# Second attention's scores in two row halves, the down product in two column halves, the second attention's keys and values in four column strips

## The reference

```python
x = x + L0_xattn(layernorm(x), ctx, ...)        # 16 heads of 16, q and k normalised per head, softmax over 1601 keys
x = x + L0_ffn(layernorm(x), U1, V1, b1, U2, V2, b2)   # 256 -> 64 -> 1024, gelu, -> 64 -> 256
x = x + L1_xattn(layernorm(x), ctx, ctx, mask, ...)    # one head of 16
x = x + L1_ffn(layernorm(x), phi, W, b)         # soft mixture over 64 experts with 32 slots each
```

```python
q = query @ Wq + bq;  k = key @ Wk + bk;  v = value @ Wv + bv
scores = einsum('bqd,bkd->bqk', q, k) / sqrt(256)
scores = (scores - mean(scores)) / (std(scores, ddof=1) + 1e-8)
attn = softmax(scores + where(mask, -1e-32, 0))
head = einsum('bqk,bkd->bqd', attn, v);  out = tile(head, 16) @ Wout + bout
```

## Time and profile before

| | us |
|---|---|
| median of three runs | 6866.95 |
| the profiled execution | 6864.03 |
| its span | 6862.2 |
| TensorE busy | 6307.0 (92%) |
| VectorE busy | 3514.3 (51%) |
| ScalarE busy | 3263.7 (48%) |
| GpSimd busy | 2408.1 (35%) |

### The profile page before, as it was taken

How to read it: one execution, slowest core, us unless ns; L and a number is a source line. 1 busy time by engine, 2 the same in 40 slices (tenths; PEclk the granted TensorE clock), 3 DMA queues, 4 the chain that set the end, 5 groups by cost and what they waited for, 6 DMA issues and landing times. The chain is left out here.

```text
span 6862.2 us, 93027 instructions
## 1 busy us (share of the span) xinstructions
PE 6307.0 (92%) x35933; PEld 3091.1 (45%) x35933; DVE 3514.3 (51%) x6804; ACT 3263.7 (48%) x6001; POOL 2408.1 (35%) x2689
## 2 busy tenths in 40 slices
PE   3799999999999999999999999966999999999999
PEld 1223333333333333333333333226888888666666
DVE  3565665665656656656656566516666666000000
ACT  1366666666666666666666666522222222111111
POOL 4226436346355264363463552342222222000000
PEclk9799999999999999999999999968999999999999
DMA  2442332432432423314324324003444444311110
GB/s 64 77 76 57 67 76 56 73 69 63 76 71 55 84 57 66 78 55 73 69 63 76 70 53 75 6 16 135 157 167 154 158 162 163 121 56 56 49 56 31
DMA packets 364938, 546.09 MB, mean 80 GB/s; under 512 B 59824, under 2 KB 281984, under 8 KB 364240
## 3 DMA queue, kind: packets, MB, share of 16 engines
q1 hardware_dynamic: 321232, 498.18, 30.0%
q10 hardware_dynamic: 43264, 41.95, 1.8%
...
## 5 line engine op out<-in xcount | busy, mean ns | idle before, releaser
L1193 DVE TENSOR_REDUCE mx<-psum 128x1 f32<-128x401 f32 x4096 | 2212.9, 570 | 1615.7 <-PE psum L767 1606.6
L1038 ACT ACTIVATE probs<-psum 128x512 f32<-128x512 f32 (+1 forms) x3328 | 1910.6, 599 | 910.4 <-PE psum L789 907.3
L767 PE MATMUL psum<-kst,qst 96*128 96x401 bf16 x4096 | 1356.6, 343 | 192.5 <-DVE mx L1193 149.6
L789 PE MATMUL psum<-qst,kst 99*128 99x512 bf16 (+1 forms) x3328 | 1286.0, 387 | 49.9 <-ACT probs L1038 44.8
L800 PE MATMUL psum<-probs,vaug 128*17 128x512 f32 x6656 | 886.8, 605 | 0.0
L789 PEld LDWEIGHTS psum<-qst,kst 99*128 99x128 bf16 (+1 forms) x3328 | 328.8, 99 | 1178.5 <-ACT probs L1038 748.9
L767 PEld LDWEIGHTS psum<-kst,qst 96*128 96x128 bf16 x4096 | 402.7, 98 | 962.8 <-DVE mx L1193 756.3
L1460 POOL TENSOR_TENSOR disp<-disp,rz 128x2048 f32<-128x2048 f32 x64 | 294.7, 4605 | 905.5 <-DVE rz L1679 905.5
L1479 PE MATMUL psum<-phi,xT 128*128 128x128 f32 x4096 | 511.0, 279 | 39.1 <-DMA xT<-xnT_scratch 31.8
L1630 ACT ACTIVATE disp<-psum 128x512 f32<-128x512 f32 x256 | 152.8, 597 | 807.6 <-PE psum L1547 807.6
L1479 PEld LDWEIGHTS psum<-phi,xT 128*128 128x128 f32 x4096 | 479.0, 193 | 86.8 <-issue 79.1
...
## 6 DMA issues: line engine op xcount, KB each, us to landing
xnb<-xn_scratch SPq DMA_DIRECT2D x256, 512.0 KB, 3.6
...
y_scratch<-ysb ACTq DMA_DIRECT2D x128, 256.0 KB, 3.3
...
```

Source lines behind the costliest of these rows:

```text
L767: mm(to[:, 0:PW], qst[g][0:NP, j, t * P:(t + 1) * P], kst[g][0:NP, j, k0:k0 + PW], start=True, stop=True).then_inc(m_full, 1)
L789: mm(bank[S_BANK[n % 2]][0:m, :], kst[g][0:NR, j, c * P:c * P + m], qst[g][0:NR, j, :], start=True, stop=True).then_inc(s_full, 1)
L1038: fn(probs[0:m, 4 * (k % 2) + j, :], bank[S_BANK[j % 2]][0:m, :], ACT.Exp, scale=float(HD) ** 0.5).then_inc(s_exp, 1)
L1193: v.tensor_reduce(mx[:, n % 2, u // 4, u % 4:u % 4 + 1], bank[M_BANK[r % 2]][:, 0:PW], AX.X, ALU.max).then_inc(m_free, 1)
```

## The change

Three products of stage one use the array in parts, and the table of `woven` is written anew from step 15 on, with smaller moves in steps 0 to 3.

1. Scores (`s1`): `kv1T` holds the keys twice, in rows 0 to 31 and 64 to 95, and `q1a` the queries twice, in rows 0 to 15 and 64 to 79. One call does two chunks: the even one with rows 0 to 63 into `hb`, the odd one with rows 64 to 127 into `b6`. A call waits for the exponentials of both chunks of the call before. Seven calls take the place of thirteen, the last with one chunk.
2. Down product (`U2`): two hidden chunks in one call, into partitions 0 to 63 and 64 to 127 of `b7`. The two halves are added by the V2 product, which has 128 rows, with V2 loaded twice.
3. Keys and values (`kv1`): four matmuls of 128 tokens for each half of the channels, in four strips of 32 partitions. ScalarE copies 128 x 128 in place of 32 x 512. The sum of the keys lies in four strips, and a new matmul with a selecting matrix `sel` (`km`) adds them up before VectorE's mean (`kmr`). The way back from DRAM is four DMAs in place of one, and GpSimd subtracts the mean from 128 partitions.

```diff
-        put((15.67, 16.34, 17.34, 18.34, 20.0, 21.0, 22.0, 23.0)[f], -1, "U2", f)
...
+    for p in range(FC // 2):
+        put((16.34, 18.34, 21.67, 23.67)[p], -1, "U2", p)
...
-    for c in range(KC):
-        put(35.0 + 0.5 * c, -1, "s1", c)
...
+    for p in range((KC + 1) // 2):
+        put((35.67, 36.67, 38.0, 39.0, 40.34, 41.34, 42.67)[p], -1, "s1", p)
     for k in range(4):
-        put((36.95, 38.95, 40.95, 41.95)[k], -1, "pv1", k)
...
-                (v2[:, :], w["L0_ffn_V2"]),
+                (v2[0:RANK, :], w["L0_ffn_V2"]),
+                (v2[RANK:P, :], w["L0_ffn_V2"]),
...
-                (bkv[0:A1, :], w["L1_xattn_bk"].rearrange("(p a) -> p a", a=1)),
-                (bkv[A1:2 * A1, :], w["L1_xattn_bv"].rearrange("(p a) -> p a", a=1)),
...
+            for j in range(4):
+                loads.append((bkv[32 * j:32 * j + A1, :], w["L1_xattn_bk"].rearrange("(p a) -> p a", a=1)))
+                loads.append((bkv[32 * j + A1:32 * j + 32, :], w["L1_xattn_bv"].rearrange("(p a) -> p a", a=1)))
...
-                    sp.wait_ge(h_full, at("h_full", b - 1, "s1", KC - 1))
+                    sp.wait_ge(h_full, at("h_full", b - 1, "s1", KC // 2))
...
-                sp.dma_start(kv1T[0:2 * A1, :], kv1_d[b]).then_inc(kv1_loaded, 16)
+                for r in (0, 64):
+                    sp.dma_start(kv1T[r:r + 32, 0:3 * S].rearrange("a (x n) -> a x n", n=P),
+                                 kv1_d[b, 0:3].rearrange("i (j a) n -> a (i j) n", j=4)).then_inc(kv1_loaded, 16)
+                    sp.dma_start(kv1T[r:r + 32, 3 * S:NK], kv1_d[b, 3][0:32, 0:NK - 3 * S]).then_inc(kv1_loaded, 16)
...
             def keys_centred(b):
...
-                pool.wait_ge(km_ready, at("km_ready", b, "km"))
-                pool.tensor_scalar(kv1T[0:A1, :], kv1T[0:A1, :], kmean[:, 0:1], None, ALU.subtract).then_inc(kc_ready, 1)
+                pool.wait_ge(km_ready, at("km_ready", b, "kmr"))
+                pool.tensor_scalar(kv1T[:, :], kv1T[:, :], kmean[:, 0:1], None, ALU.subtract).then_inc(kc_ready, 1)
...
-                    last = mm(hb[0:2 * A1, 0:m], w1kv[:, k, :], cT[:, n % 2, k, 0:m], start=(k == 0), stop=(k == 1))
+                    for j in range(-(-m // P)):
+                        w = min(P, m - j * P)
+                        last = mm(hb[32 * j:32 * j + 32, 0:w], w1kv[:, k, :], cT[:, n % 2, k, j * P:j * P + w],
+                                  start=(k == 0), stop=(k == 1), skip_group_check=True)
...
-            def ffn_down(b, f):
-                if f == 0:
+            def ffn_down(b, p):
+                if p == 0:
...
-                pe.wait_ge(g_post, at("g_post", b, "gpost", f))
-                mm(b7[0:RANK, :], u2[:, f, :], hx[:, f % 4, :], start=(f == 0), stop=(f == FC - 1)).then_inc(t_mm, 1)
+                pe.wait_ge(g_post, at("g_post", b, "gpost", 2 * p + 1))
+                for a in range(2):
+                    last = mm(b7[RANK * a:RANK * a + RANK, :], u2[:, 2 * p + a, :], hx[:, (2 * p + a) % 4, :],
+                              start=(p == 0), stop=(p == FC // 2 - 1), skip_group_check=True)
+                last.then_inc(t_mm, 1)
...
             def ffn_out(b, i):
...
-                    last = mm((b6, b7)[i][:, a * D:(a + 1) * D], pT[0:RANK, t * P:(t + 1) * P], v2[:, :], start=True,
+                    last = mm((b6, b7)[i][:, a * D:(a + 1) * D], pT[:, t * P:(t + 1) * P], v2[:, :], start=True,
...
+            def keys_mean(b):
+                pe.wait_ge(h_free, at("h_free", b, "kv1", 3))
+                if b >= 1:
+                    pe.wait_ge(t_act, at("t_act", b - 1, "xT", 3, 1))
+                mm(b6[:, 0:4], sel[:, :], ksum[:, b % 4, :], start=True, stop=True).then_inc(t_mm, 1)
+
             def layer_one_tokens(b):
...
-                if b >= 1:
-                    pe.wait_ge(t_act, at("t_act", b - 1, "xT", 3, 1))
...
-            def layer_one_scores(b, c):
-                m = key_rows(c)
-                if c % 2 == 0:
-                    head_bank(b, "s1", c)
-                    to, signal = hb, h_full
+            def layer_one_scores(b, p):
+                head_bank(b, "s1", p)
+                if p >= 1:
+                    pe.wait_ge(t_act, at("t_act", b, "s1", p - 1))
...
-                    if c >= 3:
-                        pe.wait_ge(t_act, at("t_act", b, "s1", c - 2))
-                    to, signal = b6, t_mm
-                if c == 0:
...
-                mm(to[0:m, :], kv1T[:, c * P:c * P + m], q1a, start=True, stop=True).then_inc(signal, 1)
+                c, m = 2 * p, key_rows(2 * p)
+                mm(hb[0:m, :], kv1T[0:64, c * P:c * P + m], q1a[0:64, :], start=True, stop=True).then_inc(h_full, 1)
+                if c + 1 < KC:
+                    mm(b6[:, :], kv1T[64:P, (c + 1) * P:(c + 2) * P], q1a[64:P, :], start=True,
+                       stop=True).then_inc(t_mm, 1)
...
-                fn(kv1s[:, 0:m], hb[0:2 * A1, 0:m], ACT.Identity, bias=bkv[:, 0:1],
-                   accum_out=ksum[:, b % 4, i:i + 1]).then_inc(h_free, 1)
+                r, w = (P, P) if m == S else (32, m)
+                fn(kv1s[0:r, 0:w], hb[0:r, 0:w], ACT.Identity, bias=bkv[0:r, 0:1],
+                   accum_out=ksum[0:r, b % 4, i:i + 1]).then_inc(h_free, 1)
...
             def ffn_rank_out(b):
-                act.wait_ge(t_mm, at("t_mm", b, "U2", FC - 1))
-                fn(pT[0:RANK, :], b7[0:RANK, :], ACT.Copy, scale=0.5).then_inc(t_act, 1)
+                act.wait_ge(t_mm, at("t_mm", b, "U2", FC // 2 - 1))
+                fn(pT[:, :], b7, ACT.Copy, scale=0.5).then_inc(t_act, 1)
...
-            def layer_one_exp(b, c):
-                m = key_rows(c)
+            def layer_one_exp(b, p):
+                c, m = 2 * p, key_rows(2 * p)
...
-                if c % 2 == 0:
-                    act.wait_ge(h_full, at("h_full", b, "s1", c))
-                    src, signal = hb, h_free
-                else:
-                    act.wait_ge(t_mm, at("t_mm", b, "s1", c))
-                    src, signal = b6, t_act
-                fn(hx[0:m, c % 4, :], src[0:m, :], ACT.Exp, bias=maskb[0:m, c, b:b + 1]).then_inc(signal, 1)
+                act.wait_ge(h_full, at("h_full", b, "s1", p))
+                fn(hx[0:m, c % 4, :], hb[0:m, :], ACT.Exp, bias=maskb[0:m, c, b:b + 1]).then_inc(h_free, 1)
+                if c + 1 < KC:
+                    act.wait_ge(t_mm, at("t_mm", b, "s1", p))
+                    fn(hx[:, c % 4 + 1, :], b6, ACT.Exp, bias=maskb[:, c + 1, b:b + 1]).then_inc(t_act, 1)
...
+            for j in range(4):
+                for r in (0, 64):
+                    setup(v.tensor_copy(sel[32 * j:32 * j + A1, r:r + A1],
+                                        ident[32 * j:32 * j + A1, 32 * j:32 * j + A1]))
...
             def keys_mean(b):
-                dve.wait_ge(h_free, at("h_free", b, "kv1", 3))
-                link(v.tensor_reduce(kmean[:, :], ksum[0:A1, b % 4, :], AX.X, ALU.add))
+                dve.wait_ge(t_mm, at("t_mm", b, "km"))
+                link(v.tensor_reduce(kmean[:, :], b6[:, 0:4], AX.X, ALU.add))
...
             def scale_queries(b):
...
-                v.tensor_tensor(qa[:, :, 0:A1], b6[:, A1:(QT + 1) * A1].rearrange("p (t d) -> p t d", d=A1),
-                                sg[:, :, None].broadcast_to((P, QT, A1)), ALU.mult).then_inc(t_dve, 1)
+                for r in (0, 64):
+                    ins = v.tensor_tensor(qa[:, :, r:r + A1], b6[:, A1:(QT + 1) * A1].rearrange("p (t d) -> p t d", d=A1),
+                                          sg[:, :, None].broadcast_to((P, QT, A1)), ALU.mult)
+                ins.then_inc(t_dve, 1)
...
             def scaled_queries(b):
...
-                v.tensor_copy(q1a[0:2 * A1, :], b7[0:2 * A1, :]).then_inc(t_dve, 1)
+                v.tensor_copy(q1a, b7).then_inc(t_dve, 1)
```

120 lines of the change are left out of this document (64 added, 56 removed).

## The result

| | before | after |
|---|---|---|
| median, us (5 runs each) | 6865.8 | 6830.6 |
| ratio, 95% interval | | 0.9949 [0.9934, 0.9964] |
| the profiled execution, us | 6864.0 | 6835.2 |
| its span, us | 6862.2 | 6833.3 |

The change makes the kernel 35 us faster by the medians, 29 by the two profiled executions; 76 were forecast. The range and the sign held, the size did not.

The account below looks back on a forecast made before the run. It put the whole question in the attention loop, TensorE 94% busy but handing banks to and fro with VectorE; 15 x -5.2 + 2 = -76 us gave 6788 by the profiled execution, 6791 by the median, range 6740 to 6845.

Parts of the forecast that it names:

- The pair, the strips, the down pairs: TensorE in the loop: score pair 1.15 us, keys block in strips 0.9, down pair 1.1; saving 3.1, 3.1, 4.4 a batch.
- Rival A: Loop: work removed from TensorE counts in full, 15 x 10.9 = 164 us, giving 6703; chance 0.18.
- 10.9 removed: Work taken from TensorE per batch, in us: 3.1 + 4.4 + 0.6 + 3.1 - 0.3.
- The stretches: Batch steps 0-14, 15-27, 28-34, 35-46, 47-51: forecast 85.6, 69.45, 30.95, 59.4, 19.6 us.
- gap prices: Woven work in a step's first gap costs about 0.5 us below its length, second 0.2 to 0.3, third 0.1.
- ScalarE's queue: Loop steps: two long ScalarE operations in a gap delay the fourth score or the next step's first.
- -5.2 us a batch: Whole loop batch: the five stretches' changes, -1.0 - 5.5 - 0.7 + 2.0, counted 15 times.
- 30.95 against 31.65, -0.7: Steps 28 to 34: transposes wait about 1.2 us more for GpSimd, the variance chain less; 0.7 us shorter.
- Taken as nothing either way: Tail part run once alone behind the loop, where pairs wait for both banks: no change, 0 us.
- Setup +2: Setup before the loop: seven more small loads and ten small VectorE operations add 2 us.
- Rival C: Keys' way back: keys arrive late, transposes wait 7.8 us a batch, 117 us in all, 6908; chance 0.11.
- The batch between 263 and 267: Loop batch: the prediction fails as a whole if its length lies outside 263 to 267 us.

Follow-up runs that it names:

- e4_u2ser: Changed kernel with both matmuls of a down pair on columns 0 to 63, one behind the other, and V2 of 64 rows again; 6889.0 us.
- h2_kvser: Changed kernel with the four strips of a keys block on one strip of columns, one behind the other; 6879.9 us.
- e5_rowser: Changed kernel with both scores of a pair on rows 0 to 63, one behind the other; 6922.2 us.
- e2_split: Changed kernel with the wait for a score pair's second bank moved between its two matmuls; 6828.9 us.
- h3_pairs_all: Changed kernel with split pair waits, short setup, second group's loads behind the maxima, later second-norm transposes and two widened step-30 matmuls; 6797.7 us.
- e7_slim: Changed kernel with the old number of setup loads, VectorE copying key bias and V2, small key-mean copies before its load wait; 6821.7 us.
- e1_singles: Changed kernel with row-half scores undone: 13 single scores in two banks, old table of steps 35 to 46; 6811.9 us.
- h1_before_lds: Kernel before the change with the second group's stack loads issued in step 38, behind the maxima's loads; 6858.0 us.

## Why the prediction was right in sign and wrong in size

*The pair, the strips, the down pairs.* Right or better than taken. With what stands ahead of each, the pair costs 1.06 + 0.09 = 1.15 us as taken, a block in strips 0.57 + 0.11 = 0.68 for 0.9, a down pair 1.01 + 0.11 = 1.12 for 1.1. By e4_u2ser the side-by-side running of the down pairs is worth 3.4 us a batch in the new table, nothing of it hidden, the wide V2 0.64 (forecast 0.6), the strips 2.2 by h2_kvser. Rival A is out: 3.7 undisturbed of the 10.9 removed. The Trainium skill, "TensorE: Matmul & The Clock Gate", Part 3, says that tiles in different row groups overlap and start some ns apart. The traces agree: the halves start 6 to 8 ns apart in the loop, and e5_rowser measures the overlap at 0.85 us a pair.

*The stretches.* 69.45 forecast, 69.77 measured; 59.4 and 59.10. In the second the agreement is partly luck: step 15 took 0.8 us less than its price, 23 0.7 less, 16 0.6, 25 0.7 and 27 0.9 more. In the fourth the gap prices and ScalarE's queue of the earlier trace rows worked step by step, within 0.2 us but for 45 and 46 (0.8 more, 0.45 less). There the forecast saw the loss and named its place. What it did not ask is whether the old scores could stay: single scores in that place take 57.35.

*The failed step: "-5.2 us a batch", and in it steps 28 to 34, "30.95 against 31.65, -0.7".* It compared forecast steps without disturbance with a measured batch that held a stretch at half clock. The 0.95 in the earlier trace rows said so. Undisturbed this stretch took 30.24, and afterwards 31.31: it grew by 1.1 us in place of shrinking by 0.7, with the 1.84 us wait for GpSimd in it. The five stretches, undisturbed, changed by -1.1, -5.2, +1.1, +1.7 and -0.2, together -3.7; forecast were -1.0, -5.5, -0.7, +2.0 and 0. That the forecast's own sum, 265.0, is to the tenth what was measured is luck too, as its errors of up to 0.4 cancel. Then the changed kernel lost more to disturbances than the old one, which the forecast did not price: 0.5 us, by more half clock (12 stretches against 8) and by the maxima that came late in two batches. Together 28 of the 47 us missing.

*"Taken as nothing either way": the serial part.* It was 13.6 us slower, and bounds should have been set. Single scores in two banks have one exponential under each product; a pair waits for both. 8.9 us of it are the section of scores. This comes from the pairs: with single scores it takes 22.8 to 23.4 us in all six kernels that have them, with the changed kernel's pairs and wait 30.9 to 32.2, and with the waits apart 28.2 and 29.1 (e2_split, h3_pairs_all), so that the joint wait is worth some 2 to 4. Waits and half clock come together there, and no run parts them. The other 4.7 us are open: the 120.1 ahead of the scores are 116.9 in e7_slim, which has the same calls there.

*Setup +2.* 5.2 in the pair of profiles, 5 over all runs.

*Rival C, keys late.* Out: their four loads landed in 4 to 7 us and TensorE waited for them nowhere in batches 1 to 14. A late load did hurt, but of another tensor, the maxima: in the first batch of every version with the old order of loads, in two later batches of the changed kernel, and in eight of e1_singles.

*"The batch between 263 and 267".* 265.0 undisturbed, 266.4 in the mean; that bound was too wide to fail on.

Stage two was 3.9 us longer with the same code. It held three half-clock stretches in place of two, but over all versions, none of which touches it, it takes 2190.2 to 2195.9 us (h1_before_lds 2194.2), so the difference is within what it varies by. Open is what decides in which step the clock falls: more work and a shorter wait made it rarer, wider weights did not.
